# One-core language tower on Trainium2: ScalarE copies all second-layer expert products of the last two pairs, with new slots for their feed-forward parts

## The reference, cut to what matters

```python
h = tok(x, ...)                                    # [16, 512, 64]
h = h + attn(layernorm(h), Wq, Wk, Wv, Wo)         # 8 heads, softmax over 512 keys
f = layernorm(h)
rh = relu(f @ router_w1 + router_b1)
p  = softmax(rh @ router_w2 + router_b2)           # 6 experts, the top 2 kept
h1 = relu(einsum('bsd,edh->bseh', f, expert_w1) + expert_b1)
h2 = relu(einsum('bseh,ehf->bsef', h1, expert_w2) + expert_b2)
y  = einsum('bsef,efo->bseo', h2, expert_w3) + expert_b3
out = h + sum over the top 2 of softmax(top 2 of p) * y
```

## Time and profile before

| | |
|---|---|
| median of three executions | 713.06 us |
| lowest, highest | 712.25, 714.24 us |
| the profiled execution | 712.38 us |
| its span | 710.6 us |
| TensorE busy | 653.3 us (92%) |
| VectorE busy | 554.1 us (78%) |
| ScalarE busy | 470.3 us (66%) |
| GpSimd busy | 281.1 us (40%) |
| mean granted TensorE clock | 0.986 of full |
| body 7 | about 593 to 665 us of the span |
| the tail | about 665 us to the end |

### The profile page before, as it was taken

One profiled execution on the slowest core, in us unless ns is written; L12 is line 12 of the kernel. 1 busy time (PEld: TensorE's weight loads), 2 busy tenths in 40 slices (PEclk: granted clock), 3 DMA queues, 4 the chain that ended last, 5 costly groups with the idle time before them and its releaser, 6 DMA issues.

```text
span 710.6 us, 26770 instructions
## 1 busy us (share of the span) xinstructions
PE 653.3 (92%) x11646; PEld 374.6 (53%) x11646; DVE 554.1 (78%) x1083; ACT 470.3 (66%) x1183; POOL 281.1 (40%) x354
## 2 busy tenths in 40 slices
PE   5689999999999999999999999999999999999974
PEld 5435555545655456454655455554664446554652
DVE  6678777878787887978778787878878888687566
ACT  2378885877658756786658775687558866678330
POOL 0433115403762166511953047521665119211272
PEclk9799999999999999999999999999999999999998
DMA  5000000000000000000000000000000000000001
GB/s 177 1 3 2 2 2 3 2 2 3 17 4 2 2 3 18 2 2 2 4 18 2 2 2 18 3 2 3 3 18 2 2 2 3 18 2 2 3 3 30
DMA packets 9428, 6.93 MB, mean 10 GB/s; under 512 B 8672, under 2 KB 8800, under 8 KB 9184
## 3 DMA queue, kind: packets, MB, share of 16 engines
q1 hardware_dynamic: 9312, 5.23, 2.6%
HBM read 3.13 MB, written 2.10 MB: 7 GB/s over the span
## 4 chain that ended last, share of the span: by engine, by line
PE 64%; DVE 21%; ACT 6%; issue 5%; POOL 3%; DMA 1%; SPq 0%; DVEq 0%; ACTq 0%; POOLq 0%
PE s_bank L527 25%; PE s_bank L496 19%; DVE nmax L901 7%; PE s_bank L611 4%; ACT p L788 4%; PE s_bank L686 3%; DVE e2t L1113 3%; PE s_bank L675 3%; PE s_bank L508 2%; PE s_bank L710 2%; POOL st L1202 2%; DVE st L918 2%; DVE hatt L1097 1%; PE s_bank L537 1%; PE s_bank L590 1%
## 5 line engine op out<-in xcount | busy, mean ns | idle before, releaser
L788 ACT ACTIVATE p<-s_bank,nmax 128x512 f32<-128x512 f32 x512 | 347.8, 691 | 146.3 <-DVE nmax L901 145.2
L901 DVE TENSOR_REDUCE nmax<-s_bank 128x1 f32<-128x512 f32 x512 | 325.4, 680 | 50.2 <-PE s_bank L496 49.6
L496 PE MATMUL s_bank<-kf,g 64*64 64x512 f32 x2048 | 261.0, 594 | 6.1 <-DVE y L1128 2.8
L527 PE MATMUL s_bank<-p,woz 64*64 64x256 f32 x4096 | 247.1, 378 | 9.8 <-POOL woz L347 4.4
L527 PEld LDWEIGHTS s_bank<-p,woz 64*64 64x64 f32 x4096 | 163.9, 133 | 124.4 <-issue 45.9
L347 POOL TENSOR_TENSOR woz<-cst,rz 128x256 f32<-128x256 f32 x126 | 74.5, 612 | 263.9 <-DVE rz L907 263.9
L496 PEld LDWEIGHTS s_bank<-kf,g 64*64 64x64 f32 x2048 | 74.3, 133 | 90.9 <-issue 48.1
L788 ACT ACTIVATION_READ_ACCUMULATOR p<-s_bank,nmax 128x1 f32 x512 | 105.3, 206 | 0.0
L913 DVE STREAM_TRANSPOSE m<-s_bank 128x512 f32<-128x512 f32 x64 | 45.5, 712 | 26.0 <-PE s_bank L527 26.0
L1202 POOL TENSOR_TENSOR st<-st,power 128x8 f32<-128x8 f32 x24 | 42.9, 1786 | 48.2 <-DVE st L928 48.2
L356 POOL TENSOR_TENSOR y<-y,gt 128x768 f32<-128x768 f32 x28 | 41.3, 1475 | 37.7 <-DVE gt L1081 20.7
(11 more groups left out here) (117 smaller groups left out, 514.6 us busy)
## 6 DMA issues: line engine op xcount, KB each, us to landing
tower_out<-o SPq DMA_DIRECT2D x16, 128.0 KB, 2.6
cst<-consts SPq DMA_DIRECT2D x1, 1198.0 KB, 9.2
e2t<-ids SPq DMA_DIRECT2D x1, 896.0 KB, 6.5
cst<-consts SPq DMA_DIRECT2D x1, 544.0 KB, 4.7
cst<-consts SPq DMA_DIRECT2D x1, 288.0 KB, 6.7
e2t<-ids SPq DMA_DIRECT2D x1, 128.0 KB, 2.3
cst<-consts SPq DMA_DIRECT2D x1, 4.5 KB, 2.1
```

Source lines behind the costliest of these rows:

```text
L496: last = pe.matmul(double[half(q), 512 * r:512 * r + 512], g[half(r), a // 2 % 2, a % 2, first:first + 64], kf[half(r), par, a // 4, :], s ...
L527: last = pe.matmul(bank("PV", i, a)[half(q), 512 * hh:512 * hh + 256], woz[half(r), kept, 2 * mm + hh, :], keys[:, q, :, :], start=(part = ...
L788: nc.scalar.activation(p[:, 8 * kept + c % 8, :], bank("S", i, c - r)[:, 512 * r:512 * r + 512], ACT.Exp, bias=nmax[:, c % 16:c % 16 + 1], ...
L901: nc.vector.tensor_reduce(nmax[:, c % 16:c % 16 + 1], bank("S", i, c - r)[:, 512 * r:512 * r + 512], AX.X, ALU.max, negate=True).then_inc( ...
```

## The change

ScalarE copies both halves of each `E2` bank for pairs 6 and 7, in the slots `E2_ACT`; VectorE does so for pairs 0 to 5 alone, and `e2_first` is gone. The bias products of pair 7 have slots `YB` of their own, and their banks are taken from the ring there. Nearly all slots of `Z` and `L` are new.

With the new tables TensorE's order in the tail is: Y0 of pair 6, PV part 1, PV part 2, Y1 of 6, `FIN2`, `FIN1`, Y2 of 6, Y3 of 6, bias of Y0, the warming matmuls, `T`, E1-0, `R`, `L`, E2-0, E1-1, E1-2, E2-1, E2-2, Y0, bias of Y1, Y1, bias of Y2, Y2, bias of Y3, Y3. ScalarE's is: E2-2 of pair 6, squares, xt, copy of `R`, E1-0, first exponential, E2-0, E1-1, E1-2, E2-1, second exponential, E2-2.

```diff
--- before.py
+++ after.py
@@ -92,42 +92,42 @@
 Z = {'FIN': 11,
  'LN': 11,
  'SQ': 15,
- 'LN2': 16,
- 'T': 22,
- 'T_ACT': 20,
- 'R': 23,
+ 'LN2': 17,
+ 'T': 23,
+ 'T_ACT': 22,
+ 'R': 24,
  'R_ACT': 23,
  'L': 24,
- 'GATE': (26, 26, 29, 31, 36, 42, 43),
- 'GATE_ACT': (25, 36),
- 'E1': (44, 47, 54),
- 'E1_ACT': (45, 47, 54),
- 'E2': (59, 62, 63),
- 'E2_DVE': (58, 64, 66),
- 'Y': (65, 72, 75, 77),
- 'Y_DVE': (69, 71, 74, 77)}
+ 'GATE': (25, 27, 27, 28, 36, 45, 69),
+ 'GATE_ACT': (25, 41),
+ 'E1': (40, 47, 49),
+ 'E1_ACT': (41, 47, 52),
+ 'E2': (55, 56, 63),
+ 'Y': (65, 73, 78, 82),
+ 'Y_DVE': (70, 71, 74, 76),
+ 'E2_ACT': (55, 61, 64)}
 
 
 L = {'FIN0': 63,
- 'FIN1': 0,
+ 'FIN1': 11,
  'FIN2': 9,
  'LN': 7,
  'SQ': 0,
  'LN2': 8,
- 'T': 12,
- 'T_ACT': 9,
- 'R': 13,
- 'R_ACT': 9,
- 'L': 28,
- 'GATE': (14, 24, 31, 31, 31, 37, 61),
- 'GATE_ACT': (18, 32),
- 'E1': (23, 42, 45),
- 'E1_ACT': (15, 19, 24),
- 'E2': (43, 50, 55),
- 'E2_ACT': (28, 39, 53),
- 'E2_DVE': (35, 35, 35),
- 'Y': (57, 60, 62, 63),
- 'Y_DVE': (61, 62, 63, 63)}
+ 'T': 20,
+ 'T_ACT': 0,
+ 'R': 31,
+ 'R_ACT': 2,
+ 'L': 38,
+ 'GATE': (17, 20, 21, 24, 28, 34, 52),
+ 'GATE_ACT': (11, 57),
+ 'E1': (21, 38, 40),
+ 'E1_ACT': (11, 19, 19),
+ 'E2': (38, 47, 51),
+ 'E2_ACT': (18, 37, 58),
+ 'YB': (19, 57, 63, 63),
+ 'Y': (57, 60, 63, 63),
+ 'Y_DVE': (61, 63, 63, 63)}
 
 
 
@@ -162,7 +162,7 @@
             if slot == f["E2"][e]:
                 order.append(("E2", i, e))
         for j in range(4):
-            if slot == f["Y"][j]:
+            if slot == f["YB" if f is L else "Y"][j]:
                 order.append(("Y", i, j))
 
     for slot in range(SLOTS):
@@ -219,7 +219,7 @@
     if name in ("FIN", "XT", "R", "L"):
         slot = {"FIN": f["LN"], "XT": f["T_ACT"], "R": f["R_ACT"], "L": f["GATE"][0]}[name]
     if name in ("E1", "E2", "Y"):
-        reader = "E1_ACT" if name == "E1" else "Y_DVE" if name == "Y" else "E2_DVE"
+        reader = "E1_ACT" if name == "E1" else "Y_DVE" if name == "Y" else "E2_DVE" if f is F else "E2_ACT"
         slot = f[reader][e]
     return SLOTS * (i + 1) + slot + 1
 
@@ -318,8 +318,8 @@
         ln_sq = [sem(f"ln_sq{n}") for n in range(3)]
         (tok_half, fin_ps, fin_parts, hatt_sb, x2t_ps, xt_sb, rh_ps, rh_sb, l_ps, gate, gate_act) = [
             sem(x) for x in ("tok_half", "fin_ps", "fin_parts", "hatt_sb", "x2t_ps", "xt_sb", "rh_ps", "rh_sb", "l_ps", "gate", "gate_act")]
-        (e1_ps, e1_sb, e2_ps, e2_sb, e2_first, y_ps, y_sb, y_pool, y_dve, gated) = [
-            sem(x) for x in ("e1_ps", "e1_sb", "e2_ps", "e2_sb", "e2_first", "y_ps", "y_sb", "y_pool", "y_dve", "gated")]
+        (e1_ps, e1_sb, e2_ps, e2_sb, y_ps, y_sb, y_pool, y_dve, gated) = [
+            sem(x) for x in ("e1_ps", "e1_sb", "e2_ps", "e2_sb", "y_ps", "y_sb", "y_pool", "y_dve", "gated")]
 
 
         LN_DVE, LN_STEP = 4, (4, 3, 3)
@@ -477,8 +477,6 @@
                     pe.wait_ge(e1_sb, EP * i + e + 1)
                 if name == "E2":
                     pe.wait_ge(e2_sb, EP * i + e + 1)
-                    if i + 1 == PAIRS:
-                        pe.wait_ge(e2_first, e + 1)
                 if name == "Y":
                     pe.wait_ge(y_sb, 4 * i + e + 1)
 
@@ -690,19 +688,19 @@
 
             def ffn_out(i, slot, f=F):
                 for j in range(4):
+                    double = bank("Y", i, j)
+                    if f is L and slot == f["YB"][j]:
+
+                        free("Y", i, j)
+                        for c in range(2):
+                            for q in range(2):
+                                pe.matmul(double[half(q), 512 * c:512 * c + NE * C], k("lead")[half(c), :],
+                                          k("e3b")[half(c), :], start=True, stop=False, skip_group_check=True)
                     if slot == f["Y"][j]:
-                        free("Y", i, j)
-                        double = bank("Y", i, j)
-                        if f is L:
-
-                            for c in range(2):
-                                for q in range(2):
-                                    pe.matmul(double[half(q), 512 * c:512 * c + NE * C], k("lead")[half(c), :],
-                                              k("e3b")[half(c), :], start=True, stop=False, skip_group_check=True)
+                        if f is not L:
+                            free("Y", i, j)
                         if j == 0:
                             pe.wait_ge(e2_sb, EP * i + EP)
-                            if f is L:
-                                pe.wait_ge(e2_first, EP)
                         for x in range(NE):
                             for c in range(2):
                                 for q in range(2):
@@ -835,10 +833,12 @@
                         act.wait_ge(e1_ps, EP * i + e + 1)
                         nc.scalar.activation(e1t[:, e, :], bank("E1", i, e)[:, :], ACT.Relu,
                                              bias=k("e1b")[:, e:e + 1]).then_inc(e1_sb, 1)
-                    if f is L and slot == f["E2_ACT"][e]:
+                    if f is not F and slot == f["E2_ACT"][e]:
                         act.wait_ge(e2_ps, EP * i + e + 1)
-                        nc.scalar.activation(e2t[:, 2 * e, :], bank("E2", i, e)[:, 0:512], ACT.Relu,
-                                             bias=k("e2b")[:, 2 * e:2 * e + 1]).then_inc(e2_first, 1)
+                        for r in range(2):
+                            last = nc.scalar.activation(e2t[:, 2 * e + r, :], bank("E2", i, e)[:, 512 * r:512 * r + 512],
+                                                        ACT.Relu, bias=k("e2b")[:, 2 * e + r:2 * e + r + 1])
+                        last.then_inc(e2_sb, 1)
                 if slot == f["R_ACT"]:
                     act.wait_ge(rh_ps, i + 1)
                     nc.scalar.activation(rh[:, :].rearrange("q (r x) -> q r x", r=2),
@@ -1106,10 +1106,9 @@
                     if f is L:
                         scaled(2, x2_tiles, i)
                 for e in range(EP):
-                    if slot == f["E2_DVE"][e]:
+                    if f is F and slot == f["E2_DVE"][e]:
                         dve.wait_ge(e2_ps, EP * i + e + 1)
-
-                        for r in ((1,) if f is L else (0, 1)):
+                        for r in range(2):
                             last = nc.vector.tensor_scalar(
                                 e2t[:, 2 * e + r, :], bank("E2", i, e)[:, 512 * r:512 * r + 512],
                                 k("e2b")[:, 2 * e + r:2 * e + r + 1], 0.0, ALU.add, ALU.max)
```

## The result

Twelve executions of the kernel after have a median of 710.55 us (709.40 to 712.81), twelve of the kernel before run beside them 712.40 us (710.94 to 714.24). The ratio is 0.9977, with a 95% interval of 0.9966 to 0.9988: 0.23% faster. The interval leaves out 1, so there is a gain, but it lies inside the 0.3% that I counted as no change. The forecast was 710.9 us, with 2.2 us won; 1.85 us were won between the medians. The profiled execution after took 709.40 us, with a span of 707.6 us, so the profiled pair differs by 3.0 us. That pair alone flatters the change, and the experiments say why.

What follows compares the result with a forecast made beforehand. Body 7 was taken as bound by TensorE, the tail by engines waiting for each other. Terms of minus 0.5, 0, minus 0.2 and minus 1.5 sum to minus 2.2 us: 710.9 us against the median, range 709.3 to 713.4.

Steps and rivals of the forecast that it cites:

- Step 1: Body 7: ScalarE's added copies of E2 fit into its 19.5 us without work; cost 0, at most 2.5 us.
- Step 2: Body 7, other new slots of pair 6: shorter waits less 0.3 us for an uncovered copy of `R`; minus 0.5 us.
- Step 3: Start of the tail: last PV ends 1.2 us earlier, residual sum waits 1.2 us more behind the transposition; sum 0.
- Step 4: Router and experts of pair 7: ScalarE's chain of copies replaces VectorE's ahead of Y0; minus 0.2 us.
- the absorption: Gate of pair 7: `L` comes 0.86 us later, but line 1040 still ends with GpSimd, so part 4 ends as before.
- Step 5: Last products, Y0 to Y1: granted clock stays at 2.4 GHz instead of falling to 1.2; minus 1.5 us.
- C: Rival: clock falls to 1.2 GHz ahead of pair 7's router, plus 3.1 us; total 715.5 us, chance 0.08.
- B: Rival: clock falls at the last products as before, only 0.7 us won; total 712.4 us, chance 0.37.
- D: Rival: in body 7 the exponentials fall behind ScalarE's copies and the 0.5 us is lost; 713.2 us, chance 0.10.

Runs made afterwards that it cites:

- light sums: Kernel after with GpSimd's weighted sums of pair 6's Y2 and Y3 over 4 of 64 channels; one execution, 709.39 us.
- copies alone: Kernel before with ScalarE copying both halves of E2 for pairs 6 and 7, other slots as before; median 713.00 us, ratio 1.0010.
- filled wait: Kernel before with ten warming matmuls in the wait ahead of the last pair's Y0; median 711.63 us, ratio 0.9990.
- after again: Kernel after, unchanged, run once more beside later kernels; median 709.60 us, ratio 0.9973 to the kernel before.
- the router first: Kernel after with `R` ahead of E1-0 in the tail; median 709.14 us, ratio 0.9962 to before; with warming matmuls 709.59 us, 0.9967.
- the split copy: Kernel after with `R` ahead of E1-0 and VectorE copying E2-2's second half; median 709.62 us, ratio 0.9971; with warming matmuls 708.46 us, 0.9944.

## Why the prediction was right

**Step 1** (copies in body 7, 0): right. TensorE's one listed wait for an exponential of slots 56 to 63 is the 0.15 us ahead of `FIN0`, 0.13 us more than before from start to start, and body 7 with the old slots took 61.43 us with ScalarE's copies against 61.42 without.

**Step 2** (body 7, -0.5): right in sum, -0.56. The wait ahead of the logits, 0.89 against 0.37, is the +0.5 where I had +0.3, and the wait of 0.33 at slot 44 went. It did not go by E1-0's move, as I had it: with E1-0 back at its old slot it stays away. That the gate's part 3 held up the scores is borne out by the 0.24 us that its old slots bring back.

**Step 3** (start of the tail, 0) is the step that failed. "The sum is 0" counted products alone; it was -0.92, and -0.29 more behind it. The products do cancel: `FIN1` takes 0.91 us ahead of Y0 and 0.93 behind `FIN2` (I had 1.2, the length of a record with its drain). What the step left out is the stop in the last PV, which cost 0.95 us before and is in all four profiles with `FIN1` ahead and in none of the ten with it behind. So the transposition of the last PV came 1.86 us earlier against `FIN0` (8.41 for 10.27), not 1.2. And where VectorE's centring falls against GpSimd's sum decides 0.3 us. The one slot undone gave back 0.54 and 0.30 us.

**Step 4**: the absorption was right, to 0.01 us in its end and by the light sums in its cause. Y0 was said to come 0.2 us earlier and came 0.06 later; each of the steps of ScalarE's chain had a little more latency than my sum. (In that sum 692.7 is the end of the copy of E1-1; that of E1-2 ends at 693.7, which the 693.9 of the next term covers.) That the chain replaces VectorE's as the bound is shown by the copies alone (+0.56), the exchange of `R` (-0.58) and the split of the last copy (-0.57 more).

**Step 5** (clock, -1.5): the mechanism and the size for one execution were right (-1.44), its share of the median was not. The fastest executions of before show that it does not always have the fall at Y0. The change also leaves other places where a fall can land, and one near the start lies outside of it. Adding one execution's fall in full to a median was the fault. It was made good by chance: the 1.2 us of step 3 that I had not counted stand in for it. The distances without the clock sum to 1.7 us (0.56, 0.92 and 0.29, less 0.06), against 1.85 measured between the medians, with an interval of 0.9 to 2.4. With the full 1.5 us of the clock they would sum to 3.2, outside of it; with the 0.6 that the filled wait won in the median, they sum to 2.3. What the clock gave to the median is not separated from the spread that the falls make.

**The rivals.** C, a fall ahead of the router, does happen: in single executions of after (+1.3 us), not as its rule, and in the order of before as well. It cost less than the 3.1 us I gave, because it was over before the logits and E2-0; only E1-0 and `R` ran in it. B's 712.4 us is inside the range of after, up to 712.81, but no profile except that of before has a fall at Y0. D did not happen. By its own terms (0.5 lost, 1.25 added, the clock's 1.5 won or not) it would give 712.6 to 714.1 us, not 712.1 to 713.8.

## What to carry to other kernels

Moving copies to the engine with more idle time won nothing here, because they joined a serial chain: count what that engine must do one after another between the last input and the first output, and give one late piece back to the other engine while it waits. Order steps by who waits last, and before paying to avoid a delay look for an instruction behind it that waits for another engine anyway, as line 1040 did for GpSimd. Where one profiled execution has a clock fall in it, compare it with the fastest executions of the same kernel before giving that time to the change, and compare distances between like instructions, not whole spans.

## What the runs showed of the hardware

The granted clock fell to 1.2 GHz at different places in executions of one kernel: behind T in one of after, nowhere between body 7 and the last matmul in another. Ahead of the falls near T (in after again, the router first, the copies alone and the split copy) TensorE had worked through runs of 64-row transposes and short products with waits of 0.68 to 2.32 us, never a wait as long as the 2.84 us ahead of Y0 in the kernel before. Waits of like length (0.65 to 1.60 us) stood ahead of T in profiles without a fall there. A fall cost 1.3 to 1.4 us in the distance from T to Y0 or from Y0 on, about 1 us near the start, and the long one in the profile of the split copy 2.3 us (13.30 against 10.96).

And 240 matmul records in 5.3 us, each short, were followed by a stop of 0.16 to 0.62 us behind the next matmul, with no semaphore to explain it, in four profiles of four. After 176 records in 4.4 us there was none at that place, in ten profiles of ten. Such stops are elsewhere too: after, 33 records into Y3 of pair 6, TensorE stops for 0.33 us at 678.37, where it costs nothing since `T` waits for VectorE. So the count of records is not shown to be the cause, and the cause is open.
